# Loads cut into 256 KB parts, a clip moved to GpSimd, and the norm of k moved to ScalarE in a gated cross-attention block

## The reference

```python
def _div_clamp_fp8(x, scale):
    y = jnp.clip(x / scale, -448.0, 448.0)
    return y.astype(bfloat16) -> float8_e4m3 -> float32
...
q  = _ln(fp8_linear(ln_out, wq))        # 16 heads of 128
k  = _ln(fp8_linear(ln_out, wk))        # 8 groups, 2 query heads each
v  = fp8_linear(ln_out, wv)
core = softmax(q k^T / sqrt(128)) v
qx = _ln(fp8_linear(ln_out, wqx))       # the same again over the context
kx, vx = split(cond @ w_kv_x); kx = _ln(kx)
xout = softmax(qx kx^T / sqrt(128)) vx
catq = _div_clamp_fp8(concatenate([core, xout]), proj_smooth)
x = x + tanh(g_xattn) * (catq @ wproj) * scales
...
x = x + tanh(g_ffn) * bitlinear(silu(a) * b, w_down)   # a, b = bitlinear(layernorm(x), w_gate_up)
```

## Time and profile before

| what | value |
|---|---|
| median of 3 runs | 1912.92 us (1908.5 to 1914.21) |
| the profiled execution | 1910.24 us, of which the span is 1908.4 us |
| PE busy | 1646.2 us, 86% |
| DVE busy | 1604.2 us, 84% |
| ACT busy | 1332.0 us, 70% |
| POOL busy | 999.1 us, 52% |
| first row maximum of the loop, last one | 117.9 us, 1547.2 us |

### The profile page before, as it was taken

One profiled execution on the slowest core, in us unless ns is written; L12 is line 12 of the kernel. 1 busy time (PEld: TensorE's weight loads), 2 busy tenths in 40 slices (PEclk: granted clock), 3 DMA queues, 4 the chain that ended last, 5 costly groups with the idle time before them and its releaser, 6 DMA issues.

```text
span 1908.4 us, 34982 instructions
## 1 busy us (share of the span) xinstructions
PE 1646.2 (86%) x11147; PEld 1011.0 (53%) x11164; DVE 1604.2 (84%) x3601; ACT 1332.0 (70%) x3203; POOL 999.1 (52%) x1327
## 2 busy tenths in 40 slices
PE   1368888788999998989998888999999868999996
PEld 1345555455656655556665555666666423444442
DVE  7568888998989989989998999999998846777774
ACT  6469998787879977788888777888878842222222
POOL 3566666666766666676766556666666510000000
PEclk9989998899999999999999999999999989999998
DMA  2258878679999998889999988999997877332200
GB/s 96 88 148 168 183 177 187 148 169 202 215 218 205 208 215 186 183 186 236 212 218 212 197 194 182 229 224 213 211 184 144 181 187 248 94 95 73 72 18 16
DMA packets 665435, 325.46 MB, mean 171 GB/s; under 512 B 551456, under 2 KB 594592, under 8 KB 664224
## 3 DMA queue, kind: packets, MB, share of 16 engines
q1 hardware_dynamic: 665248, 323.17, 75.2%
HBM read 140.61 MB, written 48.23 MB: 99 GB/s over the span
## 4 chain that ended last, share of the span: by engine, by line
DVE 41%; PE 27%; POOL 10%; issue 9%; ACT 8%; DMA 3%; SPq 1%; DVEq 0%; POOLq 0%; ACTq 0%
DVE nmx L946 8%; DVE pp L956 8%; PE psum L719 6%; PE psum L694 5%; PE psum L677 3%; PE psum L736 3%; PE psum L665 3%; PE psum L635 3%; DMA pt<-pp 3%; DVE cc L970 2%; DVE xh L929 2%; PE psum L642 2%; POOL qk L1507 2%; POOL ars L1485 2%; DVE ast L915 1%
## 5 line engine op out<-in xcount | busy, mean ns | idle before, releaser
L677 PE MATMUL psum<-pt,vv 128*128 128x512 f16 x1536 | 407.4, 389 | 56.7 <-ACT cy L1300 31.4
L665 PE MATMUL psum<-qk 128*128 128x512 f16 x1536 | 424.2, 386 | 18.8 <-DVE pp L956 15.8
L635 PE MATMUL psum<-wbt,xqt 128*128 128x256 f16 (+1 forms) x4096 | 411.6, 251 | 23.0 <-DVE xh L929 11.0
L1281 ACT ACTIVATE psum<-psum,nmx 128x512 f32<-128x512 f32 x512 | 341.9, 668 | 108.6 <-DVE nmx L946 105.7
L635 PEld LDWEIGHTS psum<-wbt,xqt 128*128 128x128 f16 x4096 | 334.7, 100 | 133.6 <-issue 14.7
L956 DVE SCALAR_TENSOR_TENSOR pp<-psum,prs,pp 128x512 f16<-128x512 f32 x512 | 378.0, 738 | 18.1 <-ACT pp L1292 18.1
L946 DVE TENSOR_REDUCE nmx<-psum 128x1 f32<-128x512 f32 x512 | 343.2, 670 | 32.7 <-PE psum L665 31.9
L1292 ACT ACTIVATE pp<-psum,prs 128x512 f16<-128x512 f32 x512 | 353.7, 691 | 23.6 <-DMA pt<-pp 23.6
L677 PEld LDWEIGHTS psum<-pt,vv 128*128 128x128 f16 x1536 | 149.3, 99 | 257.7 <-issue 76.9
L1507 POOL TENSOR_TENSOR qk<-y,qk 128x512 f16<-128x512 f32 x192 | 233.2, 1215 | 16.0
L665 PEld LDWEIGHTS psum<-qk 128*128 128x128 f16 x1536 | 146.2, 99 | 100.9 <-DVE pp L956 20.5
(11 more groups left out here) (171 smaller groups left out, 2704.3 us busy)
## 6 DMA issues: line engine op xcount, KB each, us to landing
wbt<-ws SPq DMA_DIRECT2D x192, 256.0 KB, 3.7
ws<-wbt SPq DMA_DIRECT2D x64, 256.0 KB, 3.9
catd<-cy SPq DMA_DIRECT2D x64, 256.0 KB, 3.3
raw<-in_wgu SPq DMA_DIRECT2D x64, 256.0 KB, 3.7
wbt<-catd SPq DMA_DIRECT2D x8, 2048.0 KB, 9.8
raw<-in_w SPq DMA_DIRECT2D x32, 384.0 KB, 3.9
pt<-pp SPq DMA_TRANSPOSE x512, 3.7
raw<-in_wp SPq DMA_DIRECT2D x32, 256.0 KB, 3.6
```

Of the source, the lines that this page charges most:

```text
L635: ins = e.matmul(bank[:, o0:o0 + c1 - c0], xv[:, v, kt * 512 + tt * 128:kt * 512 + (tt + 1) * 128], wb[i][:, h, kt, c0:c1], start=kt == 0 ...
L665: ins = e.matmul(SB(n), qk[i][:, jq, u, ss], qk[i][:, jk, w, :], start=k == 0, stop=k == 2)
L677: ins = e.matmul(OB, v[:, t, u, att, :], src[:, w, t, :], start=t == 0 and k == 0, stop=t == 3 and k == 2)
L1281: e.activation(SB(n), SB(n), ACT.Exp, bias=nmx[:, k], accum_out=psm[:, k]).then_inc(s["exp"], 1)
```

## The change

Four edits are made.

1. `load_cat(0)`, `load_cat(1)` and the two halves of `load_wg` are cut into eight parts of 256 KB each. One part is issued per slot: `wgs` in slots 444 to 451 and 488 to 495, `cat` 0 in 472 to 479, `cat` 1 in 496 to 503; `x2` follows in 506 and 507. Before, `cat` 0 was issued in slot 496, the `wgs` halves in 499 and 508, and `cat` 1 behind the loop, 2 MB each.
2. The clip of the outputs moves from DVE to POOL, in the slot in which it stood. DVE's field step, one slot later, waits for it (`o_c`).
3. From tile 36 on (group 9, `ACT_NORM`), `norm_b` is done by ACT as two instructions of 128x128, counted by a new semaphore `b_na`; all who waited for `b_n` wait for both.
4. `HEAD_ORDER` turns query head 0 first and k second.

```diff
-HEAD_ORDER = [4, 0, 1, 5, 2, 3]
+HEAD_ORDER = [0, 4, 1, 5, 2, 3]
+ACT_NORM = 9 * 4
+WG_AT, CAT_AT, X2_AT = (444, 488), (472, 496), 506
+def wait_b_n(q, tiles):
+    q.wait_ge("b_n", min(tiles, ACT_NORM))
+    q.wait_ge("b_na", tiles - ACT_NORM)
 # SP
+            def load_cat_part(u, k):
+                q.wait_ge("gb", (NIT - 1 + u) * 4)
+                ...
+                e.dma_start(cat[u][:, 4 * k:4 * k + 4, :], catd[0][:, 4 * k:4 * k + 4, u * 256:(u + 1) * 256]).then_inc(
+                    s[f"cat_ld{u}"], 16)
-            def load_wg(i):
-                q.wait_ge("gb", (NIT - NG * (1 - i)) * 4)
+            def load_wg(c):
+                q.wait_ge("gb", (NIT - NG * (c < 8)) * 4)
                 ...
-                if n == NSLOT - SLOTS:
-                    q.wait_ge("gb", (NIT - 1) * 4)
-                    load_cat(0)
-                elif n == NSLOT - SLOTS + 3:
-                    load_wg(0)
-                elif n == NSLOT - SLOTS + 12:
-                    ...
-                    load_wg(1)
+                for i in range(2):
+                    if 0 <= n - WG_AT[i] < 8:
+                        load_wg(8 * i + n - WG_AT[i])
+                    if 0 <= n - CAT_AT[i] < 8:
+                        load_cat_part(i, n - CAT_AT[i])
+                    if n == X2_AT + i:
+                        ...
+                        load_x2(i)
             weights_over(q)
-            load_cat(1)
 # DVE, out_step
-                q.wait_ge("o_y", 2 * pair + 2)
-                q.wait_ge("o_w", 4 * pair + step)
+                q.wait_ge("o_c", pair + 1)
+                q.wait_ge("o_w", 3 * pair + step)
-                if step == 0:
-                    ins = e.tensor_scalar(y, y, 448.0, -448.0, ALU.min, ALU.max)
 # DVE, norms
-                    else:
+                    elif it * 4 + tt < ACT_NORM:
                         norm_b(it, tt)
                         v_lo(it, tt)
+                    else:
+                        v_lo(it, tt)
 # ACT
+            def norm_b(it, tt):
+                n = it * 4 + tt
+                q.wait_ge("vx_lo", n + 1)
+                q.wait_ge("b_rs", n + 1)
+                q.wait_ge("hd_tr", (it - 1) * 6)
+                bank = psum[:, BANK["B", n], :]
+                e.activation(xh[it % 2][:, tt, 4, :], bank[:, 0:128], ACT.Copy, scale=brs[n % 2][:, 1, 0:1])
+                e.activation(xh[it % 2][:, tt, 5, :], bank[:, 256:384], ACT.Copy,
+                             scale=brs[n % 2][:, 1, 1:2]).then_inc(s["b_na"], 1)
 # POOL
+            def out_clip(pair):
+                y = cy[pair % 3][:]
+                q.wait_ge("o_y", 2 * pair + 2)
+                e.tensor_scalar(y, y, 448.0, -448.0, ALU.min, ALU.max).then_inc(s["o_c"], 1)
```

More of the change, by code:

```diff
@@ L257 @@
     "cx_pt cxp cxs cxw cxf cx_md cx_hi cx_lo wxp wxs wxw wxf wx_pt wm wc w_hi w_dn gf "
-    "ga gb vh vx_lo a_st b_st a_rs b_rs a_n b_n hd_tr y32 hd_hi hd_lo "
-    "scores mx exp rc sc hi lo tr0 tr1 tr2 tr3 pv o_y o_w o_q "
+    "ga gb vh vx_lo a_st b_st a_rs b_rs a_n b_n b_na hd_tr y32 hd_hi hd_lo "
+    "scores mx exp rc sc hi lo tr0 tr1 tr2 tr3 pv o_y o_c o_w o_q "
     "l_sum l_r l_ar l_sc l_t1 l_t2 l_hi l_lo l_ab l_fr l_fa flag "
@@ L375, in attention_over @@
         def attention_over(q):
+            wait_b_n(q, NIT * 4)
             for name, value in (("pv", NHC), ("o_q", NHC), ("lo", NSLOT), ("hi", NSLOT), ("exp", NSLOT),
-                                ("vx_lo", NIT * 4), ("hd_lo", NIT * 6), ("a_n", NIT * 4), ("b_n", NIT * 4),
+                                ("vx_lo", NIT * 4), ("hd_lo", NIT * 6), ("a_n", NIT * 4),
                                 ("x_q", xq_value(NB - 1, 3)),
@@ L462, in load_cat @@
                 e.dma_start(cat[u % 2][:], catd[b][:, :, h * 256:(h + 1) * 256]).then_inc(s[f"cat_ld{u % 2}"], 16)
+            def load_cat_part(u, k):
+                q.wait_ge("gb", (NIT - 1 + u) * 4)
+                for i in range(3):
+                    q.wait_ge(f"cat_st{i}", stored(NG * 2, i))
+                e.dma_start(cat[u][:, 4 * k:4 * k + 4, :], catd[0][:, 4 * k:4 * k + 4, u * 256:(u + 1) * 256]).then_inc(
+                    s[f"cat_ld{u}"], 16)
             def load_x2(T):
@@ L649, in head @@
                 bank = psum[:, BANK["T", n], :]
-                q.wait_ge("a_n" if j < 4 else "b_n", it * 4 + 4)
+                if j < 4:
+                    q.wait_ge("a_n", it * 4 + 4)
+                else:
+                    wait_b_n(q, it * 4 + 4)
                 for tt in range(4):
@@ L961, in out_step @@
                 y, tmp = cy[pair % 3][:], cc[:]
-                q.wait_ge("o_y", 2 * pair + 2)
-                q.wait_ge("o_w", 4 * pair + step)
+                q.wait_ge("o_c", pair + 1)
+                q.wait_ge("o_w", 3 * pair + step)
                 if step == 0:
-                    ins = e.tensor_scalar(y, y, 448.0, -448.0, ALU.min, ALU.max)
-                elif step == 1:
                     q.wait_ge("o_q", 2 * pair)
                     ins = e.tensor_scalar(tmp.bitcast(U16), y.bitcast(U16), 0x7F80, None, ALU.bitwise_and)
-                elif step == 2:
+                elif step == 1:
                     ins = e.tensor_scalar(tmp, tmp, 24.0, 0.375, ALU.mult, ALU.max)
@@ L1157, in dve_program @@
                     tiles(at)
-                for k, step in enumerate(("clip", "field", "step", "add")):
+                for k, step in enumerate(("field", "step", "add")):
                     for pair in pairs_at(n, OUT_AT[step]):
@@ L1355, in act_program @@
                         v_hi(it, tt)
+                for it, tt, half in tiles_at(n - 2):
+                    if half == 1 and it * 4 + tt >= ACT_NORM:
+                        norm_b(it, tt)
                 for it, o in heads_at(n):
@@ L1490, in rstd_b @@
                 q.wait_ge("b_st", n + 1)
-                q.wait_ge("b_n", n - 1)
+                wait_b_n(q, n - 1)
                 q.wait_ge("gf", it + 1)
@@ L1548, in pool_program @@
                     head_lo(it, o)
+                for pair in pairs_at(n, OUT_AT["clip"]):
+                    out_clip(pair)
                 for k in range(2):
```

20 lines of the change are left out of this document (9 added, 11 removed).

## The result

The changed kernel takes 1902.81 us in the median (1897.62 to 1904.09), the kernel before 1913.43 in the same comparison (1908.5 to 1915.96): a ratio of 0.9941, 95% interval 0.9927 to 0.9955. A second comparison gave 1899.16 against 1909.64, 0.9948 (0.9931 to 0.9965). So it is faster, by 10.6 us, where I had forecast 31. The sign was right and the size a third. The time lies at the upper end of the stated range (1866 to 1903) and outside the forecast's own (1870 to 1893).

The account below looks back on a forecast made before the run. DVE and PE were taken to bound the loop in turns, DVE alone in groups 12, 13, 20 and 21, and DMA stops its end; 16.8 us in the body and 14.2 at the end made 31, so 1882 us, range 1866 to 1903.

Parts of the forecast that it names:

- the end: Last slots: `pp` waits of 17.5 us go, 2 back from PE's clock, less 3.5, 1 and 0.8 of costs: 14.2 us gained.
- The 24 us: Loads in parts: by the skill's batching rule 24 us would be lost for each two MB; the prediction didn't follow it.
- So 0 where ACT is in step: PE's wait for ACT's norm pair: PE has 2.3 us to do first, ACT needs 1.4, so no cost.
- the body: Stretch before the end, groups of the attention loop: a gain of 16.8 us in all from clip and norm leaving DVE.
- rival 3: Slots with `cy` write and norm together, twelve groups: ACT becomes late, 38 us lost, 1937 in all; chance 0.06.
- of which I take 8.5: Groups 12, 13, 20, 21, bound by DVE alone: 2.47 us less DVE work each, 9.9, of which 8.5 gained.
- a term of 6: Groups 23 to 26: PE's floor allows 8.5 us, ACT is close behind, so 6 gained.
- 4 to 6: Clip moved from DVE to GpSimd: alone predicted to make the kernel 4 to 6 us faster.
- The price of 2: Port contention: GpSimd's clips hold up DVE instructions on SBUF, 45 us at most, taken as a loss of 2.
- taken at -2: Groups 0 to 8 lose clips only, DVE at 92% in 4 and 5: 2 us gained.
- Rival 1: Body gives nothing, only the end does, as PE, ACT and DMA are full in groups 23 to 26: 1901; chance 0.12.
- Rival 2: End gives little: slots from 488 run at DMA's pace, 12 us instead of 3.5, and 444 to 447 cost 5: 1896; chance 0.12.

## Why the prediction was right in sign and wrong in size

**The loads: right.** Forecast for the end: 17.5 + 2 - 3.5 - 1 - 0.8 = 14.2. Measured -12.2 in the changed kernel and -14.3 with the loads alone, 17 us in the median of that comparison. The argument held in its parts: the long stops are gone (longest wait of `pp` 2.8 instead of 8.7), a part lands in 3.4 to 4.0 us, the clock behind slot 496 rose to 0.90, group 30 pays 2.0, groups 27 and 28 together 0.1 with the loads alone and 0.9 in the changed kernel. The whole loads at early places, which gave nothing that can be told, exclude that the early place alone did it. The Trainium skill (DMA: Bandwidth & Descriptors, Bandwidth) would batch to 1 MiB and more; by the runs here the parts of 256 KB gave 0.991 and the whole loads of 2 MB at the same places 0.9988, since the transposes behind them counted and nobody waited for the parts. (The 24 us that the prediction puts on that rule for each 2 MB don't come out of its own rows: eight times 3.7 less 9.8 is 20. Nothing else was built on it.)

**The norm, "So 0 where ACT is in step": the step that failed.** I compared 2.3 us of PE's own work with 1.4 us of ACT's and concluded that ACT is in step. ACT wasn't: it was busy for 90% in groups 9 and 10 before, and for 142.0 of 165.1 us in 15 to 18, and the bank stays taken until its pair is done, which comes after DVE's `vx_lo` and behind the write of `cy`. In the trace ACT has no idle time ahead of any of the 92 pairs: each starts only 0.86 to 3.12 us after the end of its `vx_lo` (half of them above 0.88), against 0.29 to 2.55 (half above 0.30) with the pair in front of the write. The head wait rose by 24.0 us with the pair alone, 15.3 in the changed kernel; in groups 9, 10 and 15 to 18, where a gain of about 2 was forecast, the changed kernel lost 9.2 (the norm alone 7.0). That is more than half of the 20 us that the body missed. Part of it is TensorE's clock: over groups 15 to 18 PE stood without work for 7.9 us instead of 5.3, and its busy time rose from 159.8 to 163.0 at a mean clock of 0.98 instead of 1.00 (again 163.0 and 0.98 in the second profile). Three of the 5.8 us that these groups lost are thus slower matmuls. That the longer waits brought the clock down is likely, not shown: with the pair last the same groups had 11.1 us without work at a clock of 1.00. The three places of the pair in the slot, with the head wait and the time in step, show that this queueing costs time where ACT's added work is the same in all three. They don't show that it is all of the loss: beside clip and loads the place accounts for 4.0 of the 9.2 us and for 6.7 of the 9.3 by which the changed kernel lies above the one without the norm. Whether the rest is ACT's load or the bank that waits for DVE's `vx_lo` first is open. It is rival 3's mechanism, in place and cause; its price was 15 to 24 us of head wait instead of 38, and beside the loads it didn't make the whole slower. I gave it 0.06 because PE was at 98% in groups 9 and 10 before. That was the state with the bank freed by DVE, and said nothing about one in which ACT frees it.

**Groups 12, 13, 20 and 21, "of which I take 8.5": the second step that failed.** They gave 2.7. I read DVE at 99% as 99% of its own work. In groups 20 and 21 the norm alone took 8 x 0.409 = 3.27 us off DVE, and 2.47 came back in instructions whose number did not change. By lines (mean ns behind the comma), before and with the norm alone:

```profile
L988 DVE TENSOR_SCALAR raw<-raw 128x512 bf16<-128x512 bf16 x12 | 4.1, 343 | 0.4
...
L970 DVE TENSOR_SCALAR cc<-cc 128x1024 bf16<-128x1024 bf16 x4 | 3.4, 856 | 0.0
```

```profile
L1003 DVE TENSOR_SCALAR raw<-raw 128x512 bf16<-128x512 bf16 x12 | 5.0, 413 | 0.4
...
L985 DVE TENSOR_SCALAR cc<-cc 128x1024 bf16<-128x1024 bf16 x4 | 3.7, 923 | 0.0
```

12 x 0.070 = 0.84 and 4 x 0.067 = 0.27; the other 1.36 are in three more kinds, all SBUF to SBUF (`xqt<-xqt,xtmp` 713 to 765 ns x13, `xtmp<-xtmp` 455 to 504 x7, `xqt<-xqt` 466 to 524 x6). Those that read PSUM kept their times within 2 ns (`nmx` 669 and 670, `pp` 737 and 738, `xh<-psum,ars` 676 and 678). DVE's busy time contains what GpSimd makes it wait for. For L970 it is GpSimd's head low part: over the kernel before, 36.6 of the 43.5 us in which L970 and a GpSimd instruction run at once are with L1507, and with L1507 shortened L970 takes 0.421. `raw<-raw`, which rose to 413 ns when the norm was moved, then stays at 348, and most of the norm's move comes through in these groups. I had the hint in the earlier trace rows, 0.408 at best and 1.105 in the median, and used it only as a price of the clip. The Trainium skill (SBUF — State Buffer, SBUF: two separate sides) has GpSimd and VectorE in its two-port modes take turns at one port pair for whole instructions; the 0.856 that became 0.421 agrees.

**Groups 23 to 26, a term of 6.** Measured 3.7. The clip alone gives 5.3, the norm in front alone 2.8, both together 4.4, the norm in its place alone nothing (165.5). Two edits that relieve the same engine down to the same floor don't add up, and the norm in its place adds PE waits. **The clip** gave 11.7 where my terms made it 4 to 6, since its gain was mis-sized: the DVE clip was itself held up (31.6 us for the 64 clips, 0.493 each and not 0.416; 0.790 in the median in groups 23 to 26). The price of 2 for GpSimd's hold on DVE is not refuted; the kernel without any clip would make it 6.5, which the noise nearly covers. **Groups 0 to 8**, taken at -2, gave +0.3, and -0.6 with the clip alone; kernels whose code is the same up to there lie 1 us apart, so that little more than the missing gain can be read from it.

**The rivals.** Rival 1, a body without gain, names 1901 and the measurement is 1902.8, but by its number only: its reason was that PE, ACT and DMA are full in groups 23 to 26, and these did gain 3.7. What makes the body's zero is a gain of 6.4 in the groups where DVE was at 97% or more, less a loss of 9.2 where rival 3 had its place. Rival 2 (12 us of DMA in group 30) is excluded by 2.0.

**What stays open.** The three edits alone sum to -23.5 us in medians (-17.0, -11.7, +5.2), the change gives -10.6; in profiled spans, whose single values scatter by a few us, they sum to -9.1 and give -8.0. In medians some 13 us are lost in the combination, 9 of them already between loads and clip (-17.0 and -11.7 alone, -19.8 together). In groups 23 to 26 the three alone sum to -4.7 and the change gives -3.7, which is 1 of the 13; the rest is not settled. Nor is it how the 13 us of `out_sub` on 8 columns come together over the whole kernel; only groups 20 and 21 were read line by line.

## What to carry to other kernels

Before a PSUM reader is moved to another engine, ask who frees the bank then: the new reader's place in its queue is now in PE's loop, and an engine at 90% is late there even if its own work is short. A busy share of 99% on DVE is no promise that work taken off it becomes time; compare an instruction's minimum with its median in that stretch, and if they are far apart, look first at what GpSimd does at that time. A large load on the queue of small urgent transfers is cut to their size, and parts of a change are timed apart: here one of three cost half of what the other two gave.

## What the runs showed of the hardware

Held-up time shows as duration: the same clip on DVE took 0.416 us in the median of the kernel and 0.790 in groups 23 to 26, with 1.165 at most. GpSimd's clip over 128x1024 bf16 took 1.04 us, 2.5 times DVE's 0.416 at rest. DVE's `tensor_scalar` over 128x1024 bf16 took 0.856 us in the mean beside GpSimd's 1.2 us instruction and 0.421 when that was cut short, while those of DVE's instructions that read PSUM changed by 5 ns at most. Shortening 192 GpSimd instructions from a mean of 1.215 us to 0.259 gave 30 us, more than any edit of the change itself.
